# Routed tiles for the second expert layer, a table for the expert gather, and residual rows loaded in halves

## The reference, cut to what matters

```python
# L0_ffn: E = 8 experts, top 2, I = 512
logits = 30 * tanh((x @ w_gate) / 30); probs = softmax(logits); weights = probs * top2_mask
out = sum_e (silu(x @ w1[e]) * (x @ w3[e])) @ w2[e] * weights[:, e]

# L1_ffn (after a softmax attention inside it, whose output x is normalised to h)
probs = softmax(h @ w_router); combine = probs of the top 2 of 8, else 0       # I = 176
routed = sum_e (silu(h @ w_gate_e[e]) * (h @ w_up_e[e])) @ w_down_e[e] * combine[:, e]
sh = (silu(h @ w_sh_gate) * (h @ w_sh_up)) @ w_sh_down * sigmoid(h @ w_sh_eg)  # shared, 704 wide
x = x + routed + sh
```

## Time and profile before

| | us |
|---|---|
| median of 3 runs | 2632.03 (2627.54 to 2634.01) |
| the profiled execution | 2635.1 |
| its span | 2633.0 |
| PE busy | 2078.7 (79%) |
| DVE busy | 1525.1 (58%) |
| ACT busy | 1180.3 (45%) |
| POOL busy | 1044.7 (40%) |

### The profile page before, as it was taken

One profiled execution on the slowest core, in us unless ns is written; L12 is line 12 of the kernel. 1 busy time (PEld: TensorE's weight loads), 2 busy tenths in 40 slices (PEclk: granted clock), 3 DMA queues, 4 the chain that ended last, 5 costly groups with the idle time before them and its releaser, 6 DMA issues. The chain is left out here.

```text
span 2633.0 us, 45240 instructions
## 1 busy us (share of the span) xinstructions
PE 2078.7 (79%) x16876; PEld 1605.9 (61%) x16888; DVE 1525.1 (58%) x3266; ACT 1180.3 (45%) x2905; POOL 1044.7 (40%) x965
## 2 busy tenths in 40 slices
PE   8497438978887995967798577976789676779798
PEld 5365225646565874756587466865668665546686
DVE  2222642236675335787876876868778678357432
ACT  3211421126364333853566545655556555236433
POOL 0222012220002542586535864368623767100254
PEclk9698768989998997967799588996789777989799
DMA  8422013210003303321322213222122221120430
GB/s 288 132 24 48 9 39 71 25 44 2 23 2 97 142 0 70 106 73 33 113 80 78 69 50 100 89 63 81 57 89 81 67 69 65 37 55 2 126 113 16
DMA packets 138317, 179.47 MB, mean 68 GB/s; under 512 B 62048, under 2 KB 114544, under 8 KB 132992
## 3 DMA queue, kind: packets, MB, share of 16 engines
q1 hardware_dynamic: 129952, 166.46, 20.4%
q0 software_dynamic: 8160, 10.26, 2.5%
HBM read 154.52 MB, written 22.17 MB: 67 GB/s over the span
## 5 line engine op out<-in xcount | busy, mean ns | idle before, releaser
L2695 DVE SCALAR_TENSOR_TENSOR XT<-M_delta,CW_delta,XT 128x256 f32<-128x256 f32 x576 | 249.0, 495 | 67.7 <-ACT M_delta L2475 39.7
L2146 PE MATMUL PS<-XP_delta,X 128*128 128x268 f32 (+1 forms) x1024 | 247.2, 395 | 19.8 <-DMA X<-in_L_attn_b_heads 15.6
L2146 PEld LDWEIGHTS PS<-XP_delta,X 128*128 128x128 f32 x1024 | 196.0, 193 | 71.8 <-DMA X<-in_L_attn_b_heads 19.8
L1541 PE MATMUL PS<-XP_rffn,UW_rffn 128*128 128x512 f32 x816 | 195.3, 396 | 4.6 <-POOL UW_rffn L1495 4.6
L1541 PEld LDWEIGHTS PS<-XP_rffn,UW_rffn 128*128 128x128 f32 x816 | 156.4, 192 | 38.4 <-issue 5.4
L1273 ACT ACTIVATE PR_attn<-PS,NM_attn 128x256 f32<-128x256 f32 (+1 forms) x384 | 130.8, 448 | 103.5 <-DVE NM_attn L1343 103.5
L1495 POOL TENSOR_TENSOR UW_rffn<-W_rffn,UW_rffn 128x512 fp32r<-128x512 f32 x34 | 43.7, 1286 | 301.5 <-ACT UW_rffn L1602 301.5
L561 POOL DMA_INDIRECT sums<-XS_moe,token_moe x46 | 71.7, 1559 | 221.4 <-ACT XS_moe L661 207.0
L2613 ACT ACTIVATE S_delta<-S_delta,AO_delta 128x128 f32<-128x128 f32 x512 | 159.5, 393 | 0.0
L1663 DVE TENSOR_TENSOR SU_rffn<-PS,CB_rffn 128x512 f32<-128x512 f32 x68 | 47.0, 691 | 179.4 <-PE PS L1541 157.0
L2177 PE MATMUL PS<-KQ_delta,TR_delta 128*128 128x64 f32 x1024 | 133.8, 275 | 9.6 <-ACT TR_delta L2540 8.4
(11 more groups left out here) (459 smaller groups left out, 5259.5 us busy)
## 6 DMA issues: line engine op xcount, KB each, us to landing
M_delta<-gram_delta SPq DMA_DIRECT2D x32, 1280.0 KB, 6.0
X<-in_L_attn_b_heads SPq DMA_DIRECT2D x64, 512.0 KB, 3.5
EW<-in_L_ffn_w SPq DMA_DIRECT2D x24, 512.0 KB, 10.0
CB_rffn<-routes_rffn SPq DMA_DIRECT2D x20, 512.0 KB, 21.9
XN<-in_L_attn_b_outs SPq DMA_DIRECT2D x16, 512.0 KB, 3.7
F_delta<-in_L_attn_b_outs SPq DMA_DIRECT2D x4, 2048.0 KB, 9.5
W_rffn<-in_L_ffn_tiles SPq DMA_DIRECT2D x4, 1536.0 KB, 11.5
slots<-pad SPq DMA_DIRECT2D x2, 2967.0 KB, 14.1
```

The lines of the kernel that those rows point to most:

```text
L1541: last = nc.tensor.matmul(PS[:, 4 + 2 * n + q, :], UW[qw][:, r, (q * KD + k) * P:(q * KD + k + 1) * P], XP[qx][:, k, n * NB:(n + 1) * NB], ...
L2146: last = nc.tensor.matmul(PS[:, 1 + i, 0:B * (WIN - halo)], WH[:, r, i, k, :], XP[:, k, :, n * BT + halo:n * BT + WIN], start=(k == 0), st ...
L2695: nc.vector.scalar_tensor_tensor(TMP[:, r, i], RAW[:, r, i, :, tau:tau + BT], CW[:, i, h, tau:tau + 1], TMP[:, r, i], ALU.mult, ALU.add).t ...
```

## The change

Three things. First, X is loaded in two halves with a semaphore each, in `setup` and at the end of `moe`; nothing in that block waits for them, and the next `Norm` waits for a half ahead of its statistics. Second, `moe` no longer moves rows into slots. A class `Routing` builds, by 16 fp32 products of a one-hot `spread` with `entry`, a table that says for each slot which token and which weight it has; the normalised rows are stored once in DRAM, POOL gathers a tile's 128 rows by index, six tiles ahead, and the numbers of the tiles' experts come packed eight in a word of 24 bits, which PE reads as three words and takes apart with shifts and masks. Third, `routed_ffn` computes only the shared expert densely (6 tiles, in two halves of 512 tokens, with the three passes as before), and the routed experts in 23 gathered tiles in fp32, one expert a tile, between the halves. Their answers go to a DRAM table `answers`, from which POOL gathers two rows a token (16 indirect transfers); DVE adds them with their weight. The low parts of the second half's hidden rows are made by DVE and no more by POOL.

```diff
 class Norm
             h = self.half(q)
+            dve.wait_ge(self.core.x_in[q], 16 * self.loads)
...
+    def load_x(self, sp, src):
+        self.x_loads += 1
+        for q in range(2):
+            h = slice(q * NT // 2, (q + 1) * NT // 2)
+            sp.dma_start(self.X[:, h], src[:, h]).then_inc(self.x_in[q], 16)
...
 class Routing
+    def table(self, pe, spread):
+        w = (1 + self.weighted) * self.TILES
+        pe.wait_ge(self.entry_d, 1)
+        for j in range(2 * NT):
+            pe.wait_ge(self.spread_d, j // NT + 1)
+            last = nc.tensor.matmul(PS[:, 6, P:P + w], spread[:, j], self.entry[:, j].rearrange("p x t -> p (x t)"),
+                                    start=j == 0, stop=j == 2 * NT - 1)
+    def warm(self, bank, times):
+        for i in range(times):
+            nc.tensor.transpose(self.core.PS[:, bank, 0:P], self.core.ident[:], self.core.ident[:])
+    def experts(self, pe):
+        pe.wait_ge(self.owner_d, 1)
+        words = [pe.value_load(self.owner[0:1, w:w + 1], min_val=0, max_val=E ** 8 - 1) for w in range(3)]
+        return [pe.snap((words[t // 8] >> (3 * (t % 8))) & (E - 1)) for t in range(self.TILES)]
...
 def moe, SP
-            sp.wait_ge(placed, 32 * NT * (layer_no + 1))
-            for i in range(len(GROUPS) - 1):
-                at = slice(GROUPS[i], GROUPS[i + 1])
-                sp.dma_start(XS[:, at], slots[:, at]).then_inc(x_in[i], 16)
+            norm.rows_ready(sp)
+            sp.dma_start(rows, XN[:]).then_inc(rows_out, 16)
...
-            sp.dma_start(X[:], sums).then_inc(x_back, 16)
-            sp.wait_ge(x_back, 16)
+            core.load_x(sp, sums)
 def moe, POOL
-            for i in range(NT):
-                for r in range(2):
-                    nc.gpsimd.indirect_dma_start(
-                        core.slots[:], bass.IndirectOffsetOnAxis(ap=slot[:, r, i:i + 1], axis=0),
-                        XW[:, r, i], None).then_inc(placed, 16)
+            pool.wait_ge(rows_out, 16)
+            pool.wait_ge(routing.token_d, 1)
+            for t in range(AHEAD):
+                gather(t)
...
                 nc.gpsimd.indirect_dma_start(core.sums[:], ..., compute_op=ALU.add).then_inc(added, 16)
+                if t + AHEAD < TILES:
+                    gather(t + AHEAD)
 def moe, PE
+            routing.ranks(pe)
+            routing.warm(4, 20)
+            routing.table(pe, spread)
+            e = routing.experts(pe)
+            routing.warm(4, 24)
 def moe, DVE
+            routing.choose(dve, c, prob)
+            routing.place(dve, c)
+            routing.spread(dve, spread, 0)
+            routing.entries(dve, c)
+            routing.spread(dve, spread, 1)
+            routing.owners(dve, c)
+            routing.tokens(dve, c)
...
 def routed_ffn, PE
+            up(0, 0)
...
+            up(0, 1)
+            up(0, 2)
+            down(0, 0)
+            pe.wait_ge(log_d, 1)
+            routing.ranks(pe)
+            up(0, 3)
+            down(0, 1)
+            up(0, 4)
+            down(0, 2)
+            up(0, 5)
+            routing.table(pe, spread)
+            down(0, 3)
+            down(0, 4)
+            down(0, 5)
+            e = routing.experts(pe)
...
+            for t in range(3):
+                turn(t)
+            pe.wait_ge(yt_ev, KD)
+            for t in range(TILES):
+                gate_up(t)
+                if t >= 1:
+                    turn_hidden(t - 1)
+                if t + 3 < TILES:
+                    turn(t + 3)
+                if t >= 2:
+                    answer(t - 2)
...
+            up(1, 0)
+            pe.wait_ge(xk_d, TILES)
+            shared_rows(0, 6)
+            up(1, 1)
+            up(1, 2)
+            for m in range(ST):
+                down(1, m)
+                if m + 3 < ST:
+                    up(1, m + 3)
+            shared_rows(1, 2)
 def routed_ffn, POOL
+            pool.wait_ge(y_out, 16 * TILES)
+            for i in range(NT):
+                for r in range(2):
+                    nc.gpsimd.indirect_dma_start(
+                        G[:, r, i], None, answers,
+                        bass.IndirectOffsetOnAxis(ap=routing.slot[:, r, i:i + 1], axis=0)).then_inc(returned[i], 16)
 def routed_ffn, DVE
+            product(1)
+            product(2)
+            routing.place(dve, c)
+            routing.entries(dve, c)
+            product(3)
+            routing.spread(dve, spread, 0)
+            product(4)
+            routing.spread(dve, spread, 1)
...
+            for x in range(ST, 2 * ST):
+                product(x)
+                low(x)
+                if x == ST:
+                    shared(0, 6)
+                for _ in range(2 * (0, 1, 1, 2, 1, 2)[x - ST]):
+                    routed(j)
+                    j += 1
```

More of the change, by code:

```diff
@@ L472, in moe @@
     prob = s.sb("prob", [P, NT, E])
[L473 to L477, removed]
-    mx = s.sb("mx", [P, NT])
[L479 to L496, removed]
-    XS = s.sb("XS", [P, TILES, D + 2])
-    XW = s.sb("XW", [P, 2, NT, D + 2])
-    token = s.sb("token", [P, TILES], mybir.dt.uint32)
+    mx = s.sb("mx", [P, NT])
+    XS = s.sb("XS", [P, TILES, D])
+    spread = s.sb("spread", [P, 2 * NT, P])
     XK = s.sb("XK", [P, 3, KD, P])
@@ new lines, in routed_ffn @@
+    xt_mm, xk_d, gu_mm, sr_d, hr_d, th_mm, ht_d, y_mm, y_ev = (s.sem(n) for n in (
+        "xt_mm", "xk_d", "gu_mm", "sr_d", "hr_d", "th_mm", "ht_d", "y_mm", "y_ev"))
+    gathered, here = core.gathered, 16 * (core.gather_no + 1)
+    returned, back = core.returned, 32 * (core.return_no + 1)
+    core.gather_no += 1
+    core.return_no += 1
+    norm = Norm(core, s, layer=False, rms_eps=1e-6, weight=a["L1_ffn_w_ln2"], hidden=G[:, 0])
+    routing = Routing(core, s, 0, G[:, 1].rearrange("p i d -> p (i d)"))
@@ L1459, in routed_ffn @@
+    token = routing.token
+    half = lambda n: slice(n * NB, (n + 1) * NB)
     with nc.Block() as block:
@@ L1620, in hidden @@
[L1620 to L1633 removed]
+            down_high(1)
@@ L1637, in _, with shared @@
+            def shared(n, bank):
+                for i in range(4):
+                    dve.wait_ge(row_mm, 2 * n + i // 2 + 1)
+                    c.then(nc.vector.scalar_tensor_tensor(X[:, 4 * n + i, :], PS[:, bank + i // 2, (i % 2) * D:(i % 2 + 1) * D],
+                                                          gate[:, 4 * n + i], X[:, 4 * n + i, :], ALU.mult, ALU.add))
             norm.vector(dve)
             c = Chain(dve, chain_v)
-            for e in range(E):
-                last = nc.vector.memset(rank[:, e:e + 1], float(E - e))
@@ new lines, in _ @@
+            product(4)
+            routing.spread(dve, spread, 1)
+            nc.vector.tensor_copy(routing.slot[:].rearrange("p r i -> p (r i)"), routing.where[:]).then_inc(routing.slot_d, 1)
+            routing.owners(dve, c)
+            product(5)
+            low(5)
+            routing.tokens(dve, c)
+            dve.wait_ge(xh_d, 2)
+            nc.vector.tensor_tensor(XP[1][:, :, half(1)], XT[:, :, half(1)], XP[0][:, :, half(1)], ALU.subtract).then_inc(xl_d, 1)
+            for t in range(3):
+                columns(t)
```

761 lines of the change are left out of this document (447 added, 314 removed).

## The result

The changed kernel's median is 2604.9 us (2600.1 to 2606.3, 4 runs) beside 2631.03 for the kernel before: ratio 0.9898, 95% interval 0.988 to 0.9917. It is faster by 1.0%, where 3.6% was forecast, and lies 33 us above the range. The profiled execution took 2606.1 us, span 2604.5. The same kernel was measured in three more sessions (a session is one submission of a few kernels, all on one chip), at 2605.3, 2608.6 and, in one, the "quiet" one, 2547.1 us, while the kernel before stayed at 2628 to 2633 in all of them.

What follows compares the result with a forecast made beforehand. PE work was taken to bound routed_ffn, and waiting ahead of the loop moe. Savings of 6.7 (residual halves), 25.8 (moe) and 65.4 us (routed_ffn), 97.9 in all, took 2635.1 to 2537 us, range 2515 to 2572.

Steps and rivals of the forecast that it cites:

- The step that failed: In routed_ffn, gathers start at 859.3, one every 1.27 us, and stay ahead of a 57 us loop of 23 tiles.
- the returns: At the end of routed_ffn, 16 gathers bring the answer rows back in 21.5 us, beside PE's second half.
- First routed gate: In routed_ffn, the first gate product of a gathered tile comes about 52 us after the stage's start.
- The two stages: Both routed_ffn stages: 33.5 us saved in the first and 31.9 in the second, together 65.4 us.
- `moe` with the load behind it: Two moe stages: 12.9 us saved in each, 25.8 together, plus 2.3 us for each residual load behind them.
- The table: Front of moe: 16 fp32 matrix products on PE, 4.2 us at full clock, taken as 5.6 us.
- The words: Front of moe: PE reads and shifts the packed expert numbers before its transposes, taken as 2 us.
- The router in `moe`: Front of moe: the router's 32 records on PE, 4.2 us at full clock, given no change.
- The halves: Residual rows loaded in halves, at setup and after each moe: 2.1, 2.3 and 2.3 us saved, 6.7 us in all.
- Gathers do not cost what adds cost: Rival, chance 0.2: gathers hold POOL 1.55+0.3 us and land after 3.8 like adds, giving 2554 us.
- Register work: Rival, chance 0.13: 23 shifts and masks at 0.4 us on PE's path cost 7 us more per stage, 2565 us.
- The rival on the slow side: Rival, chance 0.04: slower than before because POOL's gathers, each over 2.5 us, bound routed_ffn; 2686 us at 4 us each.

Runs made afterwards that it cites:

- e6: The changed kernel unchanged, run again beside two of its versions in a quiet session: 2547.1 us, ratio 0.9678.
- e8: The changed kernel with routed_ffn's gathers paced by their use (six at once, each later one waiting for a product), in a quiet session: 2552.8 us.
- e13: The changed kernel unchanged, run beside a version with spaced gathers in a session with stalls: 2608.6 us, ratio 0.9922.
- e4: The changed kernel with the residual rows loaded by one transfer again, both halves of the norm waiting for it: 2556.0 us.
- e12: The changed kernel with a 768-column POOL fill behind most gathers and returns in routed_ffn, every 2.0 us instead of 1.25: 2561.9 us, ratio 0.9747.

## Why the prediction was wrong

**The step that failed** is in `routed_ffn`: "Gathers are on their way from 859.3 and one every 1.27 us, so they are ahead", and the same for the returns ("15 x 1.27+2.5 = 21.5"). The gathers were ahead, at 1.25 us. What was missing is a cost to others, in the sessions with stalls, to which the result's own belongs: I priced POOL's issues by POOL's time and the landing, and let 23 and then 16 of them stand beside engines that hand over to each other every 0.3 to 2 us, at no price. In the changed kernel's profile this costs 20.2 us in the loop (74.9 against 54.7 in e6) and 8.5 in the second half (173.1-134.2 = 38.9 us from its first `up` to the stage's last work, against 143.5-113.1 = 30.4 in e6), 29 in that stage, 57 in both (346.0 against 288.8), of the 68 by which the median misses the forecast. No row of before showed it. The earlier trace rows had a run of sixteen software issues at 1.27 us, but nothing beside it was handing over: PE idle for 26.93 us, the rest done. (The profile of before has the mark of the sessions with stalls too: it kept 119 and 116 of the 256 updates of these two runs.) That such a row can't show the cost is what I should have seen: the cover of a price of nothing must be seen beside busy engines.

**The rest of the steps**, held against e6, where the stall is absent; there the time, 2547.1, lies within the range, 10 above the forecast. (The sum starts from the profiled 2635.1 us; from the median, 2632.03, it would have given 2534.)
- First routed gate 55.1 us after the first statistics (56.0 after), 52 forecast: 3 us too early. Tile period 2.49 us in the full stretch (2.48). Second half started at 113.1 (112), work ended at 143.5 (141.4). The two stages gave 30.9+29.1 = 60.0 (65.4).
- `moe` with the load behind it: 14.1+16.1 = 30.2 (30.4). The sum came true in part by luck. In the first of them the first turn came 8.9 us earlier (10.5), the loop was 2.4 shorter (2.4), the rest, with the load, gave 2.8 (2.3). The table took 7.06 us at half clock (5.6 taken; of the 32 profiled `moe` fronts with a table 20 show 7.06, the others 6.3 to 7.0, so the 20 transposes ahead of it did not keep the clock up). The words cost nothing that shows: the 24 transposes follow the table at once. First turn at 35.5 us (34).
- The router in `moe` was given no new price (4.2 us). In the changed kernel and its versions it takes 4.0 to 5.0 us or 6.97. The clock falls to half 9.3 and 10.1 us after the stages' first statistics in e6, and 5.7 and 5.3 us after them in the result's profile, ahead of the router's start at 7.5. In the result's profile it is 6.97 in both stages, which is the larger part of the 6 us that `moe` lacks there; it comes in both kinds of session (e8, quiet, has it once; e13, with stalls, not at all), so it is apart from the stall.
- The halves: from the issue to the second half's statistics 2.5 us less at the start and 2.6 and 2.9 in `moe` (2.1, 2.3, 2.3), though e4 puts only 5 of these 8 us down to the split itself. At the start little of it is left at the stage's end: to `moe` it is 60.8 us in the quickest profiles and 63.6 in the slowest, 62.2 in the one of before.
- The delta stage is 1.6 to 7.9 us longer in the four profiles of the changed kernel than in the one of before, 1326 to 1335 over all runs; nothing there was changed. In e6 it is 5.1 us, and the two `routed_ffn` stages fell 5.4 short: these are nearly all of the 11 us that e6's span (2546.2) lacks.

**The rivals.** Gathers do not cost what adds cost: 0.95+0.30 us against 1.55. Beside the returns DVE's subtraction L1834 takes 0.69 to 0.75 us (median 0.693) as elsewhere, and the adds of the returned rows 0.485, quiet or not. With that the trace agrees with the second half of what the Trainium skill, "SBUF — State Buffer", section "Who interferes with whom", infers: that descriptor generation leaves `tensor_tensor` alone. Register work was not dear. The rival on the slow side had the right culprit, POOL's gathers, and the wrong mechanism: it had them too slow, above 2.5 us each, where they hurt by coming too fast.

## What to carry to other kernels

Do not send a long run of software gathers beside a loop that lives on quick handovers: six in a row cost no time in any run, twenty-three at 1.25 us cost 20 us where a session had stalls, and one every 2 us left the tile loop whole in either kind. Pace them by their use, or with a small fill on POOL; in a session with stalls that was worth 46.7 us here (e12 beside e13), and it costs up to 6 in a quiet one (e8 beside e6), of which the `routed_ffn` stages show 2. When a kernel's stall can't be explained from its program, run the kernel again unchanged, in another session, before theories are built on what a neighbouring version does.

## What was not expected of the hardware

The effect itself: PE's semaphore updates held back by up to 18.1 us, in order, once eight to ten software gathers had been issued 1.25 us apart. And that the kernel before, with two runs of sixteen such issues, kept its time within 0.2% in all sessions, while of the nine in which the changed kernel or a version of it was timed six had stalls and three had none, the chip's number 6 among both.
